# Middle attention of a four-layer kernel: the order of VectorE's work, a third buffer slot, 256-key blocks as three high/low passes, and values projected transposed

## The reference

```python
q = einsum('bth,oh->bto', x, Wq)   # 32 heads of 128
k = einsum('bth,oh->bto', x, Wk)   # 8 kv heads of 128
v = einsum('bth,oh->bto', x, Wv)
q = q * cos + _rotate_half(q) * sin
k = k * cos + _rotate_half(k) * sin
scores = einsum('bkgtd,bksd->bkgts', qg, k) * scale        # 4 query heads per kv head
scores = where(causal, scores, -inf)
attn = softmax(scores)
out = einsum('bkgts,bksd->bkgtd', attn, v)
return einsum('bto,ho->bth', out, Wo)
```

## Time and profile before

| what | value |
|---|---|
| median of 3 runs | 2086.09 us (2085.99 to 2092.09) |
| the profiled execution | 2092.34 us |
| its span, first to last instruction | 2090.4 us |
| mean granted clock of PE | 0.967 |
| PE busy over the span | 1934.0 us, 93% |
| DVE, ACT, POOL busy | 1141.7, 840.2, 830.1 us |
| the middle attention | from about 334 to 1172 us |

### The profile page before, as it was taken

One profiled execution on the slowest core, in us unless ns is written; L12 is line 12 of the kernel. 1 busy time (PEld: TensorE's weight loads), 2 busy tenths in 40 slices (PEclk: granted clock), 3 DMA queues, 4 the chain that ended last, 5 costly groups with the idle time before them and its releaser, 6 DMA issues.

```text
span 2090.4 us, 29438 instructions
## 1 busy us (share of the span) xinstructions
PE 1934.0 (93%) x10808; PEld 1280.3 (61%) x10808; DVE 1141.7 (55%) x2195; ACT 840.2 (40%) x1919; POOL 830.1 (40%) x1363
## 2 busy tenths in 40 slices
PE   6899967999999999999998899969999897999897
PEld 3454435888878888888886687844444454544343
DVE  4766466666666666666666324135555454566345
ACT  1565523444444444444444333313555402565420
POOL 1455316545454545454543444412344312343301
PEclk9999978999999999999999899989999998999998
DMA  7223000101010101010000234134333006112101
GB/s 197 39 41 105 2 11 1 51 1 51 1 51 1 51 1 51 1 51 18 34 31 1 91 104 158 45 44 50 55 62 95 31 1 77 32 33 54 45 0 40
DMA packets 46208, 94.57 MB, mean 45 GB/s; under 512 B 7689, under 2 KB 35721, under 8 KB 43145
## 3 DMA queue, kind: packets, MB, share of 16 engines
q1 hardware_dynamic: 43474, 90.34, 16.9%
q10 hardware_dynamic: 2592, 2.36, 0.8%
HBM read 61.68 MB, written 2.10 MB: 31 GB/s over the span
## 4 chain that ended last, share of the span: by engine, by line
PE 77%; DVE 11%; ACT 4%; issue 3%; DMA 2%; POOL 1%; ACTq 1%; POOLq 0%; SPq 0%; DVEq 0%
PE PS L1373 9%; PE PS L1454 9%; PE PS L452 5%; PE PS L555 5%; PE PS L1864 5%; PE PS L533 5%; PE PS L499 5%; PE PS L580 4%; PE PS L1384 3%; PE PS L1433 3%; PE PS L1877 3%; PE PS L1404 2%; PE PS L1416 2%; PE PS L1835 2%; PE PS L467 2%
## 5 line engine op out<-in xcount | busy, mean ns | idle before, releaser
L973 ACT ACTIVATE PB<-PS 128x512 f32<-128x512 f32 x480 | 280.9, 599 | 239.6 <-PE PS L533 236.7
L749 DVE TENSOR_REDUCE NM<-PS 128x2 f32<-128x1024 f32 x192 | 209.2, 1092 | 184.3 <-PE PS L501 183.4
L878 POOL TENSOR_SCALAR_AFFINE_SELECT PB<-PB 128x256 f32<-128x256 f32 (+1 forms) x480 | 173.3, 365 | 322.4 <-ACT PB L973 316.1
L499 PE MATMUL PS<-KQ 96*128 96x512 bf16 (+3 forms) x768 | 189.3, 311 | 46.1 <-DMA KQ<-LOW 31.4
L533 PE MATMUL PS<-KQ 99*128 99x512 bf16 (+3 forms) x768 | 183.7, 305 | 5.4 <-DMA KQ<-NMT 2.3
L1762 POOL TENSOR_SCALAR PR<-PR,RCP 128x512 f32<-128x512 f32 (+3 forms) x256 | 134.0, 532 | 106.8 <-DVE RCP L1562 106.7
L452 PE MATMUL PS<-XTT,WA 128*128 128x512 f32 x288 | 147.8, 621 | 13.5 <-DVE ident_masks_b L2402 12.0
L1695 ACT ACTIVATE PR<-PS,NX 128x512 f32<-128x512 f32 (+3 forms) x256 | 137.8, 538 | 42.2 <-DVE NX L1574 39.9
L1631 ACT CAST OTH<-PS 128x512 fp32r<-128x512 f32 x64 | 37.5, 586 | 289.2 <-PE PS L1438 289.2
L501 PE MATMUL PS<-ident_masks_b 128*128 128x128 bf16 x768 | 151.6, 226 | 0.0
L499 PEld LDWEIGHTS PS<-KQ 96*128 96x128 bf16 x768 | 77.3, 101 | 116.1 <-issue 57.9
(11 more groups left out here) (309 smaller groups left out, 4585.8 us busy)
## 6 DMA issues: line engine op xcount, KB each, us to landing
KQ<-HI SPq DMA_DIRECT2D x90, 128.0 KB, 3.9
KQ<-MID SPq DMA_DIRECT2D x72, 128.0 KB, 4.7
WB<-f_w SPq DMA_DIRECT2D x12, 768.0 KB, 4.4
WB<-w1o SPq DMA_DIRECT2D x8, 1024.0 KB, 7.9
WC<-f_w SPq DMA_DIRECT2D x10, 768.0 KB, 4.3
WB<-w1a SPq DMA_DIRECT2D x8, 768.0 KB, 4.4
WB<-w1b SPq DMA_DIRECT2D x8, 768.0 KB, 5.9
WA<-w SPq DMA_DIRECT2D x6, 1024.0 KB, 6.4
```

Source lines behind the costliest of these rows:

```text
L499: pe.matmul(ps, KQ[0:SR, self.query(G, h), i * P:(i + 1) * P], KQ[0:SR, self.key(G, h), 0:n], start=True, stop=False)
L749: x = dve.tensor_reduce(nm[:, h:h + 2, i], PS[:, b:b + 2, 0:(i + 1) * P], AX.X, ALU.max, negate=True)
L878: pool.affine_select(blocks, blocks, [[0, count], [1, P]], ALU.is_ge, 0.0, base=0, channel_multiplier=-1).then_inc(s16["probs_ready"].sem, 1)
L973: act.activation(PB[:, n % PBS, :], PS[:, 4 + n % 2, :], ACT.Exp, scale=self.scale)\
```

## The change

Seven edits, all in the middle attention:

1. DVE's order. `take_o` of head n - 2 now stands behind the first maximum of head n instead of `take_o(n - 1)` at the end of head n; `take_v` moves from the end of h = 0 to block 1 of h = 1, and its last step becomes `low_v` in block 2.
2. RA gets a third slot, and `rope` waits for `rope_low` one projection further back and for `sum` of the projection before the last, which frees RB.
3. Score block 2 (256 keys) and key block 2 of `weighted` use three high/low passes. High and low parts of q, of the probabilities and of the values cover three blocks of 128, whole parts one. PTF, PTH and PTL lose their second slot.
4. `project_v` multiplies the weights' high and low parts with XH and XL as the other projections do, 12 passes of 512 columns, with the head dimension on the partitions. ACT copies the bank to VTa and VTb (`take_vT`, start of h = 3; unit 0 in the prologue), and PE turns the four blocks back (`turn_v`, behind block 1 of h = 3).
5. A1H and A1L cover all 384 columns of A, as the values' weights are now split too.
6. `copy_pT` copies one whole block (t = 3) and up to three blocks of high parts.
7. SP's `load_a` no longer waits for `v_psum`; ACT's split of A waits for `vT_psum`.

Cut to its core:

```diff
...
-sb("XL_gap", [P, 256], F32, XLs)
+VTa = sb("VTa", [P, 256], F32, XLs)
...
+VTb = sb("VTb", [P, 256], F32, XLs)
...
-A1H = sb("A1H", [P, NC, 256], F32R, L1)
-A1L = sb("A1L", [P, NC, 256], F32R, L1)
+A1H = sb("A1H", [P, NC, 384], F32R, L1)
+A1L = sb("A1L", [P, NC, 384], F32R, L1)
...
-kF = sb("kF", [P, 2, 256], F32, L1)
+kF = sb("kF", [P, 2, P], F32, L1)
...
-VF = sb("VF", [P, 2, P], F32, L1)
-VH = sb("VH", [P, 2, P], F32R, L1)
-VL = sb("VL", [P, 2, P], F32R, L1)
-qF = sb("qF", [P, 3, 256], F32, L1)
-qH = sb("qH", [P, 3, 256], F32R, L1)
-qL = sb("qL", [P, 3, 256], F32R, L1)
-RA = sb("RA", [P, 2, T], F32, L1)
+VF = sb("VF", [P, P], F32, L1)
+VH = sb("VH", [P, 3, P], F32R, L1)
+VL = sb("VL", [P, 3, P], F32R, L1)
+qF = sb("qF", [P, 3, P], F32, L1)
+qH = sb("qH", [P, 3, 384], F32R, L1)
+qL = sb("qL", [P, 3, 384], F32R, L1)
+RA = sb("RA", [P, 3, T], F32, L1)
...
-PTF = sb("PTF", [P, 2, 3, P], F32, L1)
-PTH = sb("PTH", [P, 2, 7, P], F32R, L1)
-PTL = sb("PTL", [P, 2, 7, P], F32R, L1)
+PTF = sb("PTF", [P, P], F32, L1)
+PTH = sb("PTH", [P, 10, P], F32R, L1)
+PTL = sb("PTL", [P, 10, P], F32R, L1)
...
-    "exp recip norm pT_psum pT_hi pT pv oT_hi oT y added sum lower rope_hi v_hi").split()}
+    "exp recip norm pT_psum pT_hi pT pv oT_hi oT y added sum lower rope_hi v_hi vT_psum vT").split()}
...
     def project_v(self, pe, u):
...
+        XH_b, XL_b, n = XH[u % NB], XL[u % NB], 2 * P
+        for c in range(NC):
+            for i, (w, x) in enumerate(((A1H, XH_b), (A1L, XH_b), (A1H, XL_b))):
+                x = pe.matmul(PS[:, 7, :], w[:, c, n:n + P], x[:, c, :],
+                              start=(c == 0 and i == 0), stop=(c == NC - 1 and i == 2))
+        x.then_inc(s1["vT_psum"].sem, 1)
...
+    def turn_v(self, pe, u):
...
+        pe.wait_ge(s1["vT"].sem, u + 1)
...
-            for c in range(NC):
-                x = pe.matmul(PS[:, 7, t * P:(t + 1) * P], XTT[:, u % NB, c, t * P:(t + 1) * P],
-                              A1[:, c, 256:384], start=(c == 0), stop=(c == NC - 1))
+            x = pe.transpose(PS[:, 7, t * P:(t + 1) * P], (VTa, VTb)[t // 2][:, t % 2 * P:t % 2 * P + P], ident[:, :])
...
     def scores(self, pe, n, i):
...
-        if i < 2:
-            rows, keys = slice((1 - i) * P, (2 - i) * P), slice(0, w)
+        if i < 3:
+            rows, keys = slice((2 - i) * P, (3 - i) * P), slice(0, w)
...
-            pe.matmul(ps, qF[:, n % 3, w - P:w], kF[:, u % 2, 0:w], start=True, stop=False)
+            pe.matmul(ps, qF[:, n % 3, :], kF[:, u % 2, :], start=True, stop=False)
...
-        part = lambda p, j: p[:, n % 2, 4 * j:4 + 3 * j, :]
-        for j in range(2):
+        for j in range(3):
...
-                pe.matmul(PS[:, 6, j * P:T], v[:, j, :], part(PTH, j), start=(j == 0 and i == 0), stop=False)
+                pe.matmul(PS[:, 6, j * P:T], v[:, j, :], PTH[:, 4 * j:4 + 3 * j, :],
+                          start=(j == 0 and i == 0), stop=False)
+        pe.matmul(PS[:, 6, 3 * P:T], VF[:, :], PTF[:, :], start=False, stop=False)
...
-        for j in range(2):
-            pe.matmul(PS[:, 6, j * P:T], VH[:, j, :], part(PTL, j), start=False, stop=False)
-        pe.matmul(PS[:, 6, 2 * P:T], VF[:, 0, :], PTF[:, n % 2, 0:2, :], start=False, stop=False)
-        pe.matmul(PS[:, 6, 3 * P:T], VF[:, 1, :], PTF[:, n % 2, 2, :], start=False, stop=True)\
-          .then_inc(s1["pv"].sem, 1)
+        for j in range(3):
+            x = pe.matmul(PS[:, 6, j * P:T], VH[:, j, :], PTL[:, 4 * j:4 + 3 * j, :],
+                          start=False, stop=(j == 2))
+        x.then_inc(s1["pv"].sem, 1)
...
     def output(self, pe, u):
...
+        self.turn_v(pe, 0)
...
+                if h == 3 and i == 1 and u + 1 < NU:
+                    self.turn_v(pe, u + 1)
...
     def rope(self, dve, p):
...
+        if p >= 3:
+            dve.wait_ge(s1["rope"].sem, p - 2)
...
-            dve.wait_ge(s1["rope"].sem, p - 1)
+            dve.wait_ge(s1["sum"].sem, p - 1)
...
-        dve.tensor_tensor(RA[:, slot, :], ps, TAB[:, 0, :], ALU.mult)
+        dve.tensor_tensor(RA[:, p % 3, :], ps, TAB[:, 0, :], ALU.mult)
...
-            return RA[:, p % 2, :], kH[:, u % 2, :], kL[:, u % 2, :]
+            return RA[:, p % 3, :], kH[:, u % 2, :], kL[:, u % 2, :]
...
-        return RA[:, p % 2, 256:T], qH[:, slot, :], qL[:, slot, :]
+        return RA[:, p % 3, P:T], qH[:, slot, :], qL[:, slot, :]
...
     def rope_low(self, pool, p):
...
     def low_pT(self, dve, n, i):
...
+        m = min(t, 2) + 1
...
-        at, m = (slice(t, t + 4, 3), 2) if t else (slice(0, 1), 1)
-        dve.tensor_tensor(PTL[:, n % 2, at, :], PS[:, 4 + i % 2, 0:m * P].rearrange("p (j q) -> p j q", q=P),
-                          PTH[:, n % 2, at, :].bitcast(F32), ALU.subtract).then_inc(s1["pT"].sem, 1)
+        at = slice(t, t + 3 * m - 2, 3)
+        dve.tensor_tensor(PTL[:, at, :], PS[:, 4 + i % 2, 0:m * P].rearrange("p (j q) -> p j q", q=P),
+                          PTH[:, at, :].bitcast(F32), ALU.subtract).then_inc(s1["pT"].sem, 1)
...
     def take_v(self, dve, u):
...
-        dve.tensor_copy(VH[:, :, :], ps[:, 0:2, :]).then_inc(s1["v_hi"].sem, 1)
-        dve.tensor_copy(VF[:, :, :], ps[:, 2:4, :])
+        dve.tensor_copy(VH[:, :, :], ps[:, 0:3, :]).then_inc(s1["v_hi"].sem, 1)
+        dve.tensor_copy(VF[:, :], ps[:, 3, :])
...
+    def low_v(self, dve, u):
...
-        dve.tensor_tensor(VL[:, :, :], ps[:, 0:2, :], VH[:, :, :].bitcast(F32), ALU.subtract)\
+        ps = PS[:, 7, 0:3 * P].rearrange("p (t n) -> p t n", t=3)
+        dve.tensor_tensor(VL[:, :, :], ps, VH[:, :, :].bitcast(F32), ALU.subtract)\
...
     def take_o(self, dve, n):
...
+        self.rope(dve, 2)
...
-        self.rope(dve, 2)
+        self.low_v(dve, 0)
...
             for i in range(NT):
...
+                if n >= 2 and i == 0:
+                    self.take_o(dve, n - 2)
+                if h == 1 and u and i == 1:
+                    self.take_v(dve, u)
+                if h == 1 and u and i == 2:
+                    self.low_v(dve, u)
...
             if h == 1 and u:
...
-            if n:
-                self.take_o(dve, n - 1)
-            if h == 0 and u:
-                self.take_v(dve, u)
             if h == 1 and u + 1 < NU:
...
+        self.take_o(dve, GQ * NU - 2)
         for i in range(NT):
...
     def copy_pT(self, act, n, i):
...
-        ps = PS[:, 4 + i % 2, 0:(t + 1) * P].rearrange("p (j q) -> p j q", q=P)
+        m = min(t, 2) + 1
+        ps = PS[:, 4 + i % 2, :].rearrange("p (j q) -> p j q", q=P)
...
-            act.copy(PTF[:, n % 2, 1:3, :], ps[:, 2:4, :])
-        elif t == 2:
-            act.copy(PTF[:, n % 2, 0:1, :], ps[:, 2:3, :])
-        at, m = (slice(t, t + 4, 3), 2) if t else (slice(0, 1), 1)
-        act.copy(PTH[:, n % 2, at, :], ps[:, 0:m, :]).then_inc(s1["pT_hi"].sem, 1)
+            act.copy(PTF[:, :], ps[:, 3, :])
+        act.copy(PTH[:, t:t + 3 * m - 2:3, :], ps[:, 0:m, :]).then_inc(s1["pT_hi"].sem, 1)
...
+    def take_vT(self, act, u):
...
+        act.wait_ge(s1["vT_psum"].sem, u + 1)
+        act.copy(VTa[:, :], PS[:, 7, 0:256])
+        act.copy(VTb[:, :], PS[:, 7, 256:T]).then_inc(s1["vT"].sem, 1)
...
     def high_o(self, act, n):
...
-            act.copy(A1H[:, :, :], A1[:, :, 0:256]).then_inc(s1["a_hi"].sem, 1)
+                act.wait_ge(s1["vT_psum"].sem, NB * g)
+            act.copy(A1H[:, :, :], A1).then_inc(s1["a_hi"].sem, 1)
...
     def scalar(self, act):
...
+            if p == 2:
+                self.take_vT(act, 0)
...
+            u, h = divmod(n, GQ)
+            if h == 3 and u + 1 < NU:
+                self.take_vT(act, u + 1)
             for i in range(NT):
...
-            out, upper = qF[:, n % 3, :], slice(256, T)
-        a, b = RA[:, p % 2, :], RB[:, p % 2, :]
-        x = pool.tensor_tensor(out, a[:, 0:256], b[:, 0:256], ALU.add)
+            out, upper = qF[:, n % 3, :], slice(P, T)
+        a, b = RA[:, p % 3, :], RB[:, p % 2, :]
+        x = pool.tensor_tensor(out, a[:, 0:P], b[:, 0:P], ALU.add)
...
-            pool.tensor_tensor(A1L[:, :, :], A1[:, :, 0:256], A1H[:, :, :].bitcast(F32), ALU.subtract)\
+            pool.tensor_tensor(A1L[:, :, :], A1, A1H[:, :, :].bitcast(F32), ALU.subtract)\
...
     def load_a(self, sp, g):
...
-            sp.wait_ge(s1["v_psum"].sem, NB * g)
...

```

## The result

| | before | changed |
|---|---|---|
| median of 5 runs each | 2086.09 us (2085.99 to 2092.09) | 2076.1 us (2072.59 to 2077.88) |
| ratio, with its 95% interval | | 0.9943 (0.9927 to 0.9958) |
| the profiled execution, span | 2092.34, 2090.4 | 2072.59, 2070.8 |

The changed kernel is faster by some 0.6%: by 10 us between the medians and by 19.75 between the profiled executions. Forecast was 17.1. The first thing to settle is which of the two differences the change accounts for, and the trace can say, because the stage repeats. The table gives the time between the first score passes of neighbouring heads in units 1 to 14, from PE's timeline. "Even" and "odd" are units; a first row that is 0.48 to 0.51 long instead of 0.39 had waited, and its start is counted 0.09 later.

The account below looks back on a forecast made before the run. PE's own work, with a little waiting, was taken as the bound. Terms -9.7 - 5.1 - 9.0 + 9.5 + 2.8 - 5.6 = -17.1 us took the median from 2086.09 to 2069.0; range 2057 to 2083.

Parts of the forecast that it names:

- A pass of 256 columns: Score and key blocks of 256 keys: three passes of 0.118 replace 0.43, saving 9.7 us over 128 blocks.
- R1: Rival: narrow 256-column passes are dear because weight loads cannot overlap, +27.6 us, 2096.6; chance 0.09.
- Values: Value projection in h = 2, turning back in h = 3: 0.32 us saved a unit, 5.1 in 16.
- h = 1: Second head: first maximum starts when its scores end, so the 0.60 us stall goes, 9.0 us in 15.
- R3: Rival: DVE is late in h = 1 and `output` waits as long as the stall removed, +9.0, 2078.0; chance 0.16.
- h = 2: Third head: `take_o` and a wider low part delay the second maximum; the stall grows 0.63 us, +9.5 in 15.
- R2: Rival: h = 2 gets no worse, -9.5 us, partly given back at POOL's low part of Wo, 2062.7; chance 0.20.
- A1L: Odd units but the last: POOL's wider low parts make the next head's scores wait 0.4 us, +2.8 in 7.
- The end of the stage: Last head: normalizing starts 6.2 us sooner, `take_o` (0.6) now stands behind it; -5.6, bounds -2.0 and -8.6.
- R4: Rival: the end of the stage keeps its length, +3.6 to +5.6 us, 2074.6 at most; chance 0.10.
- The bound of 3.0: End of the stage: `finish` would lose 3.0 us if it got out from beside POOL's B1L; not expected.
- The third slot: RA: DVE's wait of about 3 us for POOL before rotating goes, 15 times, but no PE wait hangs on it: nothing.

Follow-up runs that it names:

- the mend: Changed kernel, but in odd units POOL forms A's low part after normalizing two blocks and forming the query's low part: 2072.0 us, ratio 0.9897.
- the second group: Second occasion and chip for follow-up runs, begun with the changed kernel unchanged: 2074.32 us beside 2092.08 for the kernel before, ratio 0.991.
- the three groups: Follow-up runs made on separate occasions and three different chips, each with the kernel before beside them: 2089.29, 2092.08 and 2088.62 us.
- the repeated run: The kernel before, run again unchanged: medians 2091.57 and 2089.29 us, ratio 1.0014.

## Why the prediction was right, point by point

The median of 2076.1 lies in the range, 7 us above the point, and the sign was right. By the trace the sum was 2.4 us too small, but this is a balance of larger misses: units 1 to 14 won 12.4 where its terms give 9.7, unit 15 won 5.8 where they give 6.8, and unit 0 won 1.35 where they give 0.3 (the last 0.3 of the sum are the values made ahead of it).

- *A pass of 256 columns*: taken as 0.118, measured 0.117. R1, with 0.163 a pass as its turning point, is out. What was loose is the statement that all of the 9.7 us is on the path: alone, the blocks won 5.4, since in h = 1 and h = 2 wider work of DVE and ACT ahead of the waits ate the rest. In the full change it came true for h = 1, whose wait had gone (-0.76 is the 0.60 of the wait and the 0.15 of the block).
- *Values*: 0.32 a unit forecast, 0.37 measured. ACT's copies were hidden, and `turn_v` did not wait.
- *h = 1*: 0.60 forecast, 0.61 measured. The values taken in this head did not delay `output`: VL ended 0.66 before it, I had 0.5. R3 is out.
- *h = 2*: this is the term that was mis-sized, +0.63 a unit forecast and +0.52 measured (12.27 to 11.88 is -0.39, and the passes give -0.91). I pushed ACT's second exponential by 0.44 and its last copy by 0.55; behind the head's first pass (724.01 before, 717.13 after) they came 0.38 and 0.50 later. The two runs that take `take_o` away from between the maxima give 0.41 to 0.46 for its part, against 0.61 of DVE's time; the rest was slack. The wait before the weighted sum became 0.77, where I had 0.9. In 15 units the term is 7.8 and not 9.5. R2, that h = 2 gets no worse, is refuted, and its side remark that even units would then give 0.4 back at POOL's low part of Wo as well: with the wait gone even units lost nothing.
- *A1L*: a wait of 0.4 in odd units only, 0.36 measured; the mend took 0.30 of it away.
- *The end of the stage*: -5.6 forecast. Unit 15 as a whole won 5.8, but 0.9 of that lies in its first two heads and 0.3 is the passes of the last two, so the end itself won some 4.5. The run with DVE's order undone says the same from the other side: 4.4. The mechanism was right. The timelines of DVE before, then of PE and DVE in the changed kernel:

```profile
1145.50 0.54 DVE L264 TENSOR_SCALAR XBB<-XBB,mv,rstd 128x512 f32<-128x512 f32 x1
```
```profile
1120.59 0.63 PE L1409 MATMUL PS<-kH,qH 128*128 128x512 f32 x1
```
```profile
1121.90 0.69 DVE L1594 TENSOR_REDUCE NX<-PS 128x1 f32<-128x512 f32 x1 [1.82 <-PE PS L1414]
...
1126.36 0.53 DVE L265 TENSOR_SCALAR XBB<-XBB,mv,rstd 128x512 f32<-128x512 f32 x1
```

The normalizing starts 5.7 us behind the last head's first pass instead of 12.0, 6.3 sooner (I had 6.2), and `finish` at 1130.51 is 3.63 long beside B1L, with `take_o` behind it. The shortfall is ahead of it: h = 2 of unit 15 took 9.08 us instead of 7.68, since PE, after waits of 1.12 and 0.73, was granted 0.52 of its clock from 1118.0 to 1121.5. In the run with two RA slots, with the same waits and full clock in that window, this head took 7.78; there the last head took longer (21.72 instead of 20.74), with 0.87 granted from 1125 to 1135. R4 is out. The bound of 3.0 for getting out from beside B1L was measured as 3.1 in the duration and 4.5 in the stage, 1.2 of it through PE's clock. The rule of the Trainium skill ("GPSIMD Engine Reference", "1. Specifications") that GpSimd shares its SBUF interfaces with Vector fits both rows.
- *The third slot*: nothing, as forecast.
- *The rate rule*: the Trainium skill's N/2.4 + 2.5 ns ("TensorE: Matmul & The Clock Gate", "Back-to-back issue gap") gives 109 ns for 256 columns, an estimate from that page. The section gives the formula for a single matmul by itself, and I used it for passes in a row. The trace has 117, and 234 for 512 against 216. The line through the case's own rows was the better guide.
- *From the sum to the median*: here the prediction was right partly by its width. It took the change off the profiled execution (2092.34) and carried that execution's distance from the median (6.25) over to the changed kernel, whose profiled execution was then 3.5 below its own median. On that occasion the medians differ by 10.0, in the second group by 17.8; the intervals of the two ratios, 0.9927 to 0.9958 and 0.9895 to 0.9926, just miss each other. The median of the kernel before was 2086.09 on the first occasion and 2089.29, 2092.08 and 2088.62 in the three groups. The trace shows where executions differ outside the change: unit 0 starts anywhere from 347.7 to 351.3 us, and from near the end of the feed-forward part behind (its last product of the weights' and the activations' high parts, 1374.11 before, 1355.28 after) to the end of the span 713.5 to 716.3 us pass. What sets these two stays open. The heads of units 1 to 14 repeat to 0.06 us, also the one head that differs from its kind in the kernel before (h = 1 of unit 5, 22.77 and in the repeated run 22.74, where the others have 22.50). Unit 0 doesn't: it took 41.12 us before and 39.77 in the changed kernel, yet 41.37 in the run with A's low part later, which leaves unit 0 as it is. The windows view of PE in these three, in this order:

```profile
356.00:360.00 4.00, 4.00 (x16) 0.58 0.00 0
```
```profile
356.00:360.00 4.00, 2.63 (x16) 1.00 0.02 4
```
```profile
356.00:360.00 4.00, 4.00 (x13) 0.50 0.02 4
```

PE had waited in the 4 us ahead of each, and with the lower clock its first head took 9.84 and 9.97 us against 7.63. So of the 19.5 us the 12.4 of units 1 to 14 are what the change did; the 7.1 of units 0 and 15 also hold what the clock of these two executions added or took.

## What to carry to other kernels

When an order of work is changed everywhere, price it at each place where it acts. Here "maxima first" won 0.6 us in one head and lost 0.4 in the next, and one condition that left the old order in that head was worth 6 us. Making PE's passes shorter wins nothing in a head that waits, if the work that ends the wait has grown with them: first move what is late, then shorten. Look at the granted clock too: a wait that leaves PE idle for some microseconds can cost more than its own length, here 3.1 us of waiting and 1.2 at the lower clock. The releaser in the row is only the last link: ACT was named in every one, and what helped was to move operations of DVE, ahead of ACT.

## What the runs showed of the hardware

- A DVE operation that reads and writes SBUF (`finish`, a tensor_scalar of 128x512 float32) took 3.63 us where a POOL tensor_tensor of 3.41 us started with it, and 0.55 without. It was held for as long as POOL's lasted.
- DVE operations that read an operand from PSUM were not held: low parts of 384 columns (PTL) took 0.56 us beside POOL's 3.50 us A1L, which starts at 689.50, and 0.55 elsewhere. They are another kind of operation than `finish`, and no run here separates the kind from the place of the operands. DVE's timeline:

```profile
690.00 0.56 DVE L1549 TENSOR_TENSOR PTL<-PS,PTH 128x384 fp32r<-128x384 f32 x1 [0.49 <-ACT PTH L1645]
```
- A wait of a few tenths of a microsecond may leave no idle mark on PE, only a first row of 0.47 to 0.50 instead of 0.40. With DVE's order undone, a wait of 0.38 before the weighted sum has none.
- After 5.39 us of idling PE's passes ran at a granted clock of 0.50, after 2.31 us at the same place at 1.00. After the same two short waits (1.12 and 0.73 us) one execution was granted 0.52 and another 1.00.
- POOL's price of a tensor_tensor grows evenly with the columns: 1.02 us at 384, 3.50 at 1536, 0.28 for each 128.
